# Mixture of experts behind attention: gated tiles transposed one tile later, next logits copied earlier, shared blocks reordered

## The reference

```
gate = xf @ router_W[j] + router_b[j]
ids = top_k(gate + gate_bias[j], 2)
weights = softmax of gate over the 2 chosen of 6 experts
h = xf @ exp_Wup + exp_bup;  h = silu(h @ exp_Wg + exp_bg) * h;  eo = h @ exp_Wdown + exp_bdown
s = (xf @ share_Wup + share_bup) in 2 parts; s = silu(s @ share_Wg + share_bg) * s; share_out = sum of s @ share_Wdown
y = xf + sum(weights * eo) + share_out
xf = y * rsqrt(mean(y * y) + 1e-6) * norm_w[j]
```

## Time and profile before

| | us |
|---|---|
| median of 3 runs | 2677.23 (2676.78 to 2680.77) |
| the profiled execution's own time | 2680.04 |
| its span, first to last instruction | 2678.3 |
| PE busy in the span | 2487.6 (93%) |
| DVE, ACT, POOL busy | 1944.4, 1780.2, 1866.1 |

### The profile page before, as it was taken

The page is one execution under the profiler, slowest core; times in us unless marked ns, Lnnn a source line. Parts: engine busy times, 40 slices in busy tenths (PEclk is TensorE's granted clock), DMA queues, the critical chain, the costliest instruction groups (busy, mean ns, idle before and its releaser), DMA issues. The chain is left out here.

```text
span 2678.3 us, 43896 instructions
## 1 busy us (share of the span) xinstructions
PE 2487.6 (93%) x12394; PEld 2068.3 (77%) x12394; DVE 1944.4 (73%) x4183; ACT 1780.2 (66%) x3874; POOL 1866.1 (70%) x1612
## 2 busy tenths in 40 slices
PE   5999999999989999999999999889998998769985
PEld 4788888888777788888888888678777877658874
DVE  7888888888887788887887888446665455764466
ACT  3788888888777788788888788733334664326652
POOL 3889989989878798898898898732263142554235
PEclk8999999999999999999999999999999999879997
DMA  3112212112111011111111111164344451225544
GB/s 76 38 39 49 45 40 43 39 29 51 40 35 36 22 27 31 25 33 30 28 30 30 23 23 23 37 189 136 112 161 143 139 183 62 63 104 182 174 139 124
DMA packets 168046, 189.60 MB, mean 71 GB/s; under 512 B 57523, under 2 KB 140345, under 8 KB 167302
## 3 DMA queue, kind: packets, MB, share of 16 engines
q1 hardware_dynamic: 154502, 152.96, 21.0%
q0 software_dynamic: 12288, 33.57, 4.0%
q10 hardware_dynamic: 1024, 0.26, 0.0%
HBM read 114.06 MB, written 81.17 MB: 73 GB/s over the span
## 5 line engine op out<-in xcount | busy, mean ns | idle before, releaser
L382 POOL TENSOR_TENSOR pl<-pr,ph 128x512 fp32r<-128x512 f32 (+1 forms) x1024 | 1300.2, 1292 | 184.1 <-ACT ph L860 167.0
L857 ACT ACTIVATE pr<-ps 128x512 f32<-128x512 f32 (+1 forms) x1152 | 664.2, 577 | 292.9 <-DVE ps L1046 148.7
L1133 DVE TENSOR_REDUCE part<-ps 128x1 f32<-128x512 f32 (+2 forms) x1152 | 697.4, 618 | 83.9 <-PE ps L571 67.9
L860 ACT ACTIVATE ph<-ps 128x512 fp32r<-128x512 f32 (+1 forms) x1152 | 664.7, 577 | 0.0
L571 PE MATMUL ps<-k_hi,q_parts 128*128 128x512 f32 (+3 forms) x1280 | 472.3, 369 | 27.3 <-DVE part L1133 10.7
L584 PE MATMUL ps<-q_parts,k_hi 128*128 128x512 f32 (+1 forms) x1152 | 442.9, 384 | 0.3 <-ACT ph L860 0.3
L585 PE MATMUL ps<-q_row,k_lo 65*128 65x512 f32 (+1 forms) x1152 | 443.1, 385 | 0.0
L571 PEld LDWEIGHTS ps<-k_hi,q_parts 128*128 128x128 f32 x1280 | 242.6, 190 | 91.6 <-DVE part L1133 19.2
L584 PEld LDWEIGHTS ps<-q_parts,k_hi 128*128 128x128 f32 x1152 | 217.0, 188 | 43.6 <-ACT ph L860 0.7
L1798 PE MATMUL ps<-exp_up,yy 128*128 x828 | 234.7, 420 | 2.3 <-ACT yy L1979 2.1
L585 PEld LDWEIGHTS ps<-q_row,k_lo 65*128 65x128 f32 x1152 | 216.9, 188 | 25.4
(11 more groups left out here) (283 smaller groups left out, 4407.9 us busy)
## 6 DMA issues: line engine op xcount, KB each, us to landing
work<-x_slots SPq DMA_DIRECT2D x138, 128.0 KB, 2.4
e_slots<-work SPq DMA_DIRECT2D x138, 128.0 KB, 1.8
y_latent<-y_sums SPq DMA_DIRECT2D x128, 128.0 KB, 2.4
yg<-y_latent SPq DMA_DIRECT2D x32, 512.0 KB, 5.1
rec<-recip_rows SPq DMA_DIRECT2D x127, 128.0 KB, 3.2
x_slots<-zero_rows SPq DMA_DIRECT2D x32, 276.0 KB, 4.0
acc_shared<-accw SPq DMA_DIRECT2D x14, 512.0 KB, 2.9
xcur<-acc_shared SPq DMA_DIRECT2D x12, 512.0 KB, 4.0
```

The lines of the kernel that those rows point to most:

```text
L382: eng.tensor_tensor(pl[:, s % RING, 0:w], pr[:, s % PR_RING, 0:w], f32(ph[:, s % RING, 0:w]), ALU.subtract).then_inc(sem, 1)
L857: act.activation(pr[:, s % PR_RING, 0:w], src, ACT.Exp).then_inc(S["probs"], 1)
L860: act.activation(ph[:, s % RING, 0:w], src, ACT.Exp).then_inc(S["probs_hi"], 1)
L1133: dve.tensor_reduce(dst, src[:, 0:w], AX.X, ALU.max).then_inc(S["max_read"], 1)
```

## The change

Four things change, all in the mixture.

1. In the tiles the gated tile is transposed one tile later: `turn_gated(t - 2)`, `tile_ghi(t - 2)`, `tile_glo(t - 2)`, and behind it `tile_down(t - 3)` and `tile_out(t - 3)`. `eg` gets a third buffer, taken from `eo`, which goes from 4 to 3. The loops run one iteration longer. Units start one iteration later (`UNITS_AT`). SP's list is the same.
2. From block 8 on, ACT copies the logits of block r + 1 ahead of `g_hi(r)` and of the squares, not behind the squares.
3. `xt_hi(r + 1)` stands ahead of `silu(r, 3)` on ACT, and `xt_lo(r + 1)` ahead of `gated(r, 3)` on DVE. `normalize` stands behind `gated(r, 2)`. In blocks 9 to 11 two of the four units stand in the middle of the block, behind `weigh`.
4. POOL's gathers stand at the start of a block, ahead of `g_lo(r)`, by a table (`GATHERS`).

```diff
+OUTS = 3
-        eg = wk[:, 6 * D:8 * D].rearrange("p (k d) -> p k d", d=D)
-        eo = wk[:, 8 * D:12 * D].rearrange("p (k d) -> p k d", d=D)
+        eg = wk[:, 6 * D:9 * D].rearrange("p (k d) -> p k d", d=D)
+        eo = wk[:, 9 * D:12 * D].rearrange("p (k d) -> p k d", d=D)
...
-                    for t in range(first, end + 2):
+                    for t in range(first, end + 3):
                         if t < end:
                             tile_up(t)
                         if t == 0:
                             shared_down(7)
-                        if t - 2 >= first:
-                            tile_down(t - 2)
-                        if first <= t - 1 < end:
-                            turn_gated(t - 1)
+                        if t - 3 >= first:
+                            tile_down(t - 3)
+                        if first <= t - 2 < end:
+                            turn_gated(t - 2)
                         if t + 2 < end:
                             turn_tile(t + 2)
...
                 def block_of(r):
-                    logits_back(r)
+                    if r <= 8:
+                        logits_back(r)
...
                     tanh(r)
                     if r not in LATE:
-                        for k in range(2, 4):
-                            silu(r, k)
+                        silu(r, 2)
                     if (r + 1) % 8:
                         xt_hi(r + 1)
+                    if r not in LATE:
+                        silu(r, 3)
+                    if r >= 8 and (r + 1) % 8:
+                        logits_back(r + 1)
                     if r not in LATE:
                         g_hi(r)
...
                         if t < end:
                             tile_silu(t)
-                        if first <= t - 1 < end:
-                            tile_ghi(t - 1)
+                        if first <= t - 2 < end:
+                            tile_ghi(t - 2)
                         if t + 2 < end:
                             tile_hi(t + 2)
                             tile_seed(t + 2)
-                        if t - 2 >= first:
-                            tile_out(t - 2)
+                        if t - 3 >= first:
+                            tile_out(t - 3)
...
+                    for u in GATHERS.get(r, ()):
+                        gather(u)
...
-                    if 8 <= r < 12:
-                        for u in range(16 + 4 * (r - 8), 20 + 4 * (r - 8)):
-                            gather(u)
...
+                def units(r, at, to):
+
+                    for u in range(16 + 4 * (r - 9) + at, 16 + 4 * (r - 9) + to):
+                        add_first(u)
+                        add_second(u)
...
-                    if 10 <= r < 14:
-                        normalize(r - 6)
+                    if 9 <= r < 12:
+                        units(r, 0, 2)
...
                     if r not in LATE:
                         gated(r, 2)
-                        gated(r, 3)
+                    if 10 <= r < 14:
+                        normalize(r - 6)
                     if (r + 1) % 8:
                         xt_lo(r + 1)
+                    if r not in LATE:
+                        gated(r, 3)
...
-                        for u in range(16 + 4 * (r - 9), 20 + 4 * (r - 9)):
-                            add_first(u)
-                            add_second(u)
+                        units(r, 2 if r < 12 else 0, 4)
                         variance(r - 5)
...
-                        if first <= t - 1:
-                            tile_glo(t - 1)
+                        if first <= t - 2:
+                            tile_glo(t - 2)
...
+GATHERS = {8: range(16, 20), 9: range(20, 22), 10: range(22, 26), 11: range(26, 30), 12: range(30, 32)}
-UNITS_AT = [FIRST_DONE + 4 + 13 * u // 8 for u in range(JT)]
+UNITS_AT = [FIRST_DONE + 5 + 13 * u // 8 for u in range(JT)]
```

More of the change, by code:

```diff
@@ L1458, in store_tile @@
                     sp.wait_ge(S["t_out"], t + 1)
-                    sp.dma_start(e_slots[s * P:(s + 1) * P, :], eo[:, t % 4]).then_inc(S[f"eo_stored{t % 4}"], DMA)
+                    sp.dma_start(e_slots[s * P:(s + 1) * P, :], eo[:, t % OUTS]).then_inc(S[f"eo_stored{t % OUTS}"], DMA)
                 def load_acc(r):
@@ L1810, in turn_gated @@
                     for it in range(2):
-                        mm = pe.transpose(ps[:, TG + t % 2, it * P:(it + 1) * P], eg[:, t % 2, it * P:(it + 1) * P], ident[:, :])
+                        mm = pe.transpose(ps[:, TG + t % 2, it * P:(it + 1) * P], eg[:, t % 3, it * P:(it + 1) * P], ident[:, :])
                     mm.then_inc(S["t_turned"], 1)
@@ L2010, in tile_out @@
                     act.wait_ge(S["t_down"], t + 1)
-                    if t >= 4:
-                        act.wait_ge(S[f"eo_stored{t % 4}"], DMA * (t // 4))
-                    act.activation(eo[:, t % 4, :], ps[:, TD + t % 2, 0:D], ACT.Copy).then_inc(S["t_out"], 1)
+                    if t >= OUTS:
+                        act.wait_ge(S[f"eo_stored{t % OUTS}"], DMA * (t // OUTS))
+                    act.activation(eo[:, t % OUTS, :], ps[:, TD + t % 2, 0:D], ACT.Copy).then_inc(S["t_out"], 1)
                 def square(u):
@@ L2115, in gather @@
                         done = TILES * (g // 2) + (TILES if g % 2 else FIRST_DONE)
-                        for k in range(4):
-                            pool.wait_ge(S[f"eo_stored{k}"], DMA * len([t for t in range(done) if t % 4 == k]))
+                        for k in range(OUTS):
+                            pool.wait_ge(S[f"eo_stored{k}"], DMA * len([t for t in range(done) if t % OUTS == k]))
                     if 4 <= u < 3 * JT:
@@ L2419, in gated @@
                         done = TILES if r == 8 else 2 * TILES
-                        for i in range(4):
-                            dve.wait_ge(S[f"eo_stored{i}"], DMA * len([t for t in range(done) if t % 4 == i]))
+                        for i in range(OUTS):
+                            dve.wait_ge(S[f"eo_stored{i}"], DMA * len([t for t in range(done) if t % OUTS == i]))
                     dve.scalar_tensor_tensor(out=out, in0=ps[:, 2 * (k % 2), :], scalar=W["share_b_up2"][:, k:k + 1], in1=ss[:, k, :],
@@ L2601, in tile_gated @@
                     dve.wait_ge(S["t_silu"], t + 1)
[L2602 to L2604 removed]
+                    if t >= 3:
+                        dve.wait_ge(S["t_turned"], t - 2)
+                    dve.tensor_tensor(eg[:, t % 3, :], ps[:, TU + t % 2, 0:I], es[:, t % 2, :], ALU.mult).then_inc(S["t_g"], 1)
                 def tile_glo(t):
@@ L2614, in tiles @@
                     tile_lo(first + 1)
-                    for t in range(first, end + 1):
+                    for t in range(first, end + 2):
                         if t < end:
@@ L2678, in late_lo, with late_units @@
                         dve.tensor_tensor(gg[:, 1, m, :], g0[:, m, :], f32(gg[:, 0, m, :]), ALU.subtract).then_inc(S["g_lo"], 1)
-                def units(us):
+                def late_units(us):
                     for u in us:
@@ L2687, in _ @@
                 gated(14, 0)
-                units((48,))
+                late_units((48,))
                 gated(14, 1)
-                units((49,))
+                late_units((49,))
                 gated(14, 2)
-                units((50,))
+                late_units((50,))
                 gated(14, 3)
@@ L2696, in _ @@
                 late_lo(14)
-                units((51, 52))
+                late_units((51, 52))
                 gated(15, 0)
-                units((53,))
+                late_units((53,))
                 gated(15, 1)
                 variance(12)
-                units((54,))
+                late_units((54,))
                 gated(15, 2)
@@ L2707, in _ @@
                 late_lo(15)
-                units((55,))
+                late_units((55,))
                 take_shared(14)
@@ L2711, in _ @@
                 variance(13)
-                units((56, 57))
+                late_units((56, 57))
                 take_shared(15)
-                units((58, 59))
+                late_units((58, 59))
                 normalize(13)
                 variance(14)
-                units((60, 61))
+                late_units((60, 61))
                 normalize(14)
-                units((62, 63))
+                late_units((62, 63))
                 variance(15)
```

2 lines of the change are left out of this document (1 added, 1 removed).

## The result

The changed kernel takes 2702.4 us (median of four runs, 2700.3 to 2704.5); the kernel before, on the same chip, 2679.0 (2676.8 to 2680.9). The ratio is 1.0088, with an interval of 1.007 to 1.0105: slower by 0.9%. The forecast was 2687, in a range of 2668 to 2700; the sign is right, the loss is more than twice what was forecast, and the time lies outside the range. The profiled execution has a span of 2698.5 us against 2678.3 before: 20.2 us more, where the forecast was 10.

What follows compares the result with a forecast made beforehand. PE, busy for 93% of the span, left only gaps and slow stretches; in blocks 10 to 12 DVE's list would bound next. Blocks -16, tail +2 and loads +24 made +10 us: 2690 profiled, 2687 against the median, range 2668 to 2700.

Steps and rivals of the forecast that it cites:

- The blocks, -16: Blocks 8 to 15: with the logits' copy early, DVE's list sets the period; 16 us off, bounds 12 to 20.
- The gathers cost nothing: POOL in the blocks: gathers ahead of the low parts were costed at nothing.
- No gain from the later transpose: Tiles: PE never waits for the gated tile's transpose, and the stalls behind a `normalize` stay; no gain.
- rival (c): Tiles: the later transpose frees PE of the `normalize` stalls, 5 us, with loads in time: 2660; chance 0.03.
- The loads, +24: Tiles: loads issued one iteration later against their transposes cost 27 us, less about 3 of overlap: 24, bounds 5 to 35.
- The tail, +2: End of each tile stage: three waits of 0.98 us instead of two, +1 us a round, +2 in all.
- The end, 0: The stretch behind the second tiles: the forecast's sum held no term for it.
- The forecast's own corner: Whole kernel: the blocks gain only 12 us and the loads lose 35, which gives 2702.
- (a): Tiles: loads land in time, only register points cost, 8 us or less: 2669, faster; chance 0.22.
- (b): Tiles: late loads cost about what the blocks give, 9 to 19 us: within 0.2% of 2677; chance 0.2.
- (d): Blocks 10 to 12: POOL's low parts late behind waiting gathers, 2 us each on top of the forecast: 2693; chance 0.05.

Runs made afterwards that it cites:

- e1: The kernel before with the new order in the blocks alone, tiles as before; 2660.8 us, ratio 0.9933.
- e7: The kernel before with only the earlier copy of the next block's logits on ACT, ahead of the squares; 2668.1 us, ratio 0.9959.
- e11: e1 with POOL's gathers left in their old place, behind the low parts and scatters of a block; 2665.2 us, ratio 0.9944.
- e9: The changed kernel with each tile's store issued two places later among SP's loads; 2659.4 us, ratio 0.9928.
- e3: The changed kernel with each tile's store issued one place later among SP's loads; 2666.7 us, ratio 0.9958.
- e4: The kernel before with each tile's store issued one place sooner among SP's loads; 2705.4 us, ratio 1.0097.
- e2: The kernel before with the tiles' later transpose and three output buffers alone, blocks in the old order; 2715.3 us, ratio 1.0135.
- e6: e1 with each tile's store issued one place later among SP's loads; 2653.3 us, ratio 0.9900.
- e12: e1 with each tile's store issued two places later among SP's loads; 2650.3 us, ratio 0.9898.
- e5: The kernel before with each tile's store issued one place later among SP's loads; 2670.6 us, ratio 0.9964.

## Why the prediction was wrong in size and right in sign

- **The blocks, -16: right, measured -14.6** (-15.4 in e1). The mechanism is the one given: DVE's list sets the period, the copy alone is worth half (e7). Of its parts, blocks 10 and 11 gained 5.7 and 5.3 us for 4.9 each, block 9 2.3 (the forecast's 3.1 without its earlier start), block 12 0.6 for nothing, and from block 13 on 2.4 (37.7 us against 40.1) for about 4. Up to block 9 1.6 us were lost where 0.8 was to be gained: half of it from the first `gated` of block 8 to that of block 9, 17.41 us against 16.55. One step was wrong without effect on the sum: POOL's scatters and SP's loads behind them were to decide the start of the second tiles. They come 14.0 us earlier, but the first load has landed by 2399.7, and the transpose at 2401.11 waited for DVE's `ranks`.
- **The gathers cost nothing: right, but for too weak a reason.** I asked only whether they delay the low parts. Left behind, they would have cost 2 us of the blocks' time, since `normalize` needs what POOL computes behind them (e11).
- **No gain from the later transpose: right.** e9 shows the same waits behind a `normalize`; rival (c) is out.
- **The loads, +24: the mechanism right (e3, e4), the term mis-sized.** The waits for loads grew by 32.2 - 9.0 = 23.2 us, where the list was forecast to grow by 27. The step that failed is the one from a wait to its cost: I took a late microsecond for a lost one and took 3 off for overlap with other stalls. Adding up what each iteration with a late load takes beyond 2.66 us gives 37.4 us against 8.9 before: 28.5 for 23.2 listed, again about 0.2 us more for each of 25 late loads, in 23 of them at a full granted clock. All other iterations together, the start of the stages among them, take 1.9 us less: that is all the overlap there was. So the term is 26.6 where 24 was forecast. That its list came out near was partly luck. The medians 3.2 and 3.6 of the earlier trace rows that it was worked out from are those of 4 of the 16 and 6 of the 25 loads (all of them give 3.6 and 3.2); the stretch 2480 to 2550, priced at 7 us, has 3.8 us of waits, while the first tiles ahead of 2150, priced only by their register points, have 9.3 in nine places against 2.3 in one before.
- **The tail, +2: the term that failed most for its size.** An added iteration at the drained end was priced at its one wait of 0.98 us; it costs its work too. From the last `turn_tile` to the end of the stage the changed kernel needs 14.2 us (2239.92 to 2254.16) against 10.3 in the first tiles, 3.9 more, with the clock at 0.50 at the end; in the second tiles, at the full clock, 2.5 more: 6.4.
- **The end, 0: measured +1.5.** It's left open. PE's list of waits there is the same in both kernels, and its busy time 33.7 us against 32.0. It doesn't go with the change in the tiles: e2, e3, e4 and e9 show 64.9 to 65.1 us, but so do e6 and e12 with the tiles of before (65.2 and 65.1), and e1 and e5 show 63.6 and 63.5.

Together: 28.5 + 6.4 - 1.9 = 33.0 us for the tiles (18.8 + 14.3 by the windows), against 26; with -14.6 for the blocks and 1.7 for the end and the start 20.2 us, against 10. The forecast's own corner, 12 us gained and 35 lost, gave 2702: the bounds held, but I let the range end at 2700. Of the 15 us between 2687 and 2702 these terms are 10; the rest is that the kernel before came out 1.8 us slower beside the changed one than the 2677.23 of the forecast, and that its profiled execution lay above its median and the changed kernel's below.

**The rivals.** (a), the loads land in time, fell with the 32.2 us of waits; the medians of all loads are 3.2 and 3.3 us in two of the three stretches, its own limit of about 3. The rule that I had cited from the Trainium skill, DMA: Bandwidth & Descriptors, section Anatomy of one DMA, gives an estimate of 2.3 us for such a load. The section states it for DMAs that GpSimd issues, and these are issued by SP; the trace agrees with it in the best stretch (a median of 2.3 over all its loads) and not in the other two (3.2 and 3.3). (b), late loads cost 9 to 19 us, fell by size. That neighbours share a stall does occur: 39 loads take over 3.2 us and 25 waits are listed, and two of 7.1 and 6.4 us (issued at 2464.8 and 2466.2) make one wait of 5.5. (d), late low parts on POOL, shows in no row of blocks 10 to 12. PE's one wait at `shared_down`, in block 14, was forecast to shrink by up to 1.5 us and grew from 3.9 to 4.8 (5.5 with the gathers left behind).

## What to carry to other kernels

When a pipeline gets a stage deeper, list every queue that carries both its output and the next input: here a load stood behind a store that waited for the output, so a deeper pipeline took a whole tile from the loads' margin, and moving the store one place back in the list gave back more than the change had lost. Before a margin is cut, compare it with the slow half of the landing times, not with their median. Before a spread of landing times is used, see how many loads it covers. And price a drained iteration at all that it holds (work, wait, perhaps a slower clock), and many short waits at a little more than their listed time.

## What the runs showed of the hardware

- Late loads cost PE a little more than the profile lists: in e4 24.4 us of stage for 19.7 more us of listed waits, in the changed kernel 28.5 for 23.2, about 0.2 us for each late load. For four long waits in the kernel before, 9.0 us listed, it is 8.9.
- In the tail of the changed kernel's first tiles the pairs of products take 0.40 to 0.43 us behind the first gap of about 1 us and 0.63 to 0.69 behind the second and the third (2248.90, 2252.20), where the granted clock is 0.50; over the last 14 us of the stage its mean is 0.81. In the second tiles the same three gaps leave it at 1.00.

```profile
2239.90:2254.16 14.26, 10.80 (x59) 0.81 0.16 56
```

- Landing times of equal loads (128 KB) lie between 2.0 and 7.4 us in one execution (the kernel before, all 138 by their semaphores' records: median 2.4). The long ones stand largely behind larger transfers of the same queue (25 of 43, against 14 of the 95 others, over 3.2 us). A margin of 3.3 us was missed 23 to 26 times in 138, one of 6.0 us 4 or 5 times.
